# Attention in one kernel: score banks read in pairs, maxima read one bank at a time, VectorE turning the maxima

## The reference, cut to what matters

```python
q, k, v = (split_heads(binlinear(x, W, b)) for W, b in ((Wq, bq), (Wk, bk), (Wv, bv)))
att = jnp.einsum('bhtd,bhsd->bhts', q, k) * 8 ** -0.5
att = jax.nn.softmax(att, axis=-1)
y = jnp.einsum('bhts,bhsd->bhtd', att, v)
return binlinear(y.transpose(0, 2, 1, 3).reshape(8, 512, 128), Wp, bp)
```

## Time and profile before

| | us |
|---|---|
| median of 3 runs | 989.87 |
| lowest and highest | 982.49, 992.93 |
| the profiled execution | 992.35 |
| its span | 990.5 |
| attention of layer 0 in the span | about 30 to 439 |

### The profile page before, as it was taken

How to read it: one execution, slowest core, us unless ns; L and a number is a source line. 1 busy time by engine, 2 the same in 40 slices (tenths; PEclk the granted TensorE clock), 3 DMA queues, 4 the chain that set the end, 5 groups by cost and what they waited for, 6 DMA issues and landing times. The chain is left out here.

```text
span 990.5 us, 18391 instructions
## 1 busy us (share of the span) xinstructions
PE 897.2 (91%) x6674; PEld 461.9 (47%) x6674; DVE 695.5 (70%) x1054; ACT 634.7 (64%) x1383; POOL 366.1 (37%) x355
## 2 busy tenths in 40 slices
PE   4699999999999999979998989899769999999997
PEld 2333444344434344448888878332223444444443
DVE  7879888898989999613333338878867767766654
ACT  4468677778777878852322222476557778777875
POOL 4013030214343333005556542255645547554300
PEclk9579899999999999989999989999789999999999
DMA  7615525140414000036766553259977999999800
GB/s 226 250 39 207 230 71 211 40 162 27 176 45 151 28 26 25 8 98 181 209 198 199 164 176 96 54 111 136 144 88 75 108 110 101 103 104 112 92 12 22
DMA packets 80973, 114.30 MB, mean 115 GB/s; under 512 B 12946, under 2 KB 58004, under 8 KB 78452
## 3 DMA queue, kind: packets, MB, share of 16 engines
q1 hardware_dynamic: 73684, 94.87, 48.2%
q0 software_dynamic: 6352, 17.86, 5.3%
q10 hardware_dynamic: 848, 0.40, 0.1%
HBM read 56.00 MB, written 33.57 MB: 90 GB/s over the span
## 5 line engine op out<-in xcount | busy, mean ns | idle before, releaser
L989 DVE TENSOR_REDUCE a_nmax<-quad 128x2 f32<-128x1024 f32 x256 | 302.1, 1220 | 32.4 <-PE quad L603 29.9
L798 ACT ACTIVATE a_probs<-bank 128x512 f32<-128x512 f32 x339 | 190.8, 598 | 53.0 <-PE bank L620 36.9
L1873 ACT ACTIVATE a_late<-quad 128x256 f32<-128x256 f32 (+3 forms) x512 | 180.4, 461 | 37.3 <-PE quad L1642 36.6
L2028 DVE SCALAR_TENSOR_TENSOR a_late<-a_late,const 128x512 f32<-128x512 f32 x128 | 117.8, 928 | 73.8 <-ACT a_late L1873 73.5
L632 PE MATMUL av<-a_probs,a_va 128*32 128x256 f32 x2048 | 166.1, 397 | 0.9 <-ACT a_probs L798 0.6
L603 PE MATMUL quad<-k_stack,q_stack 24*128 24x512 f32 x512 | 133.6, 523 | 9.9 <-DVE a_nmax L989 5.8
L620 PE MATMUL bank<-q_stack,k_stack 26*128 26x512 f32 x339 | 136.8, 504 | 2.8 <-DMA q_stack<-a_nparts 2.0
L798 ACT ACTIVATE a_probs<-misc 128x512 f32<-128x512 f32 x173 | 103.4, 598 | 28.9 <-PE bank L620 16.2
L1642 PE MATMUL quad<-q_stack,k_stack 96*128 96x256 bf16 (+3 forms) x512 | 104.1, 305 | 7.4 <-ACT a_late L1873 3.7
L1653 PE MATMUL av<-a_late,a_va 128*32 128x512 f32 (+3 forms) x1024 | 96.1, 448 | 8.1 <-DVE a_late L2039 7.1
L508 POOL DMA_INDIRECT sorted_rows<-x_rows,a_slot x64 | 62.4, 974 | 107.5 <-PE av L632 105.0
(11 more groups left out here) (304 smaller groups left out, 1406.1 us busy)
## 6 DMA issues: line engine op xcount, KB each, us to landing
spread<-a_parts SPq DMA_DIRECT2D x48, 256.0 KB
q_stack<-a_parts SPq DMA_DIRECT2D x96, 128.0 KB, 7.4
k_stack<-a_parts SPq DMA_DIRECT2D x96, 128.0 KB, 7.8
wu<-packed_weights SPq DMA_DIRECT2D x20, 384.0 KB
m_wu<-packed_weights SPq DMA_DIRECT2D x19, 384.0 KB
q_stack<-spread SPq DMA_DIRECT2D x7, 1024.0 KB
k_stack<-spread SPq DMA_DIRECT2D x7, 1024.0 KB
sorted_rows<-in_shape_constants POOLq DMA_DIRECT2D x5, 1040.0 KB, 5.4
```

Source lines behind the costliest of these rows:

```text
L798: act.activation(probs[:, (GH * s + j) % 8, :], col_bank(n)[:, :], ACT.Exp, scale=scale).then_inc(col_free, 1)
L989: dve.tensor_reduce(nmax[quad % 2][:, at:at + 2 * TT:TT], row_slot(n)[:, :, :], AX_X, ALU.max, negate=True)\
L1873: act.activation(probs[:, (64 * b + n) % 12, kt * P:T], quad[:, n % 4, kt * P:T], ACT.Square, bias=1.0, scale=0.25)\
L2028: dve.scalar_tensor_tensor(out=blocks, in0=blocks, scalar=1.0, in1=S["tri"][:, None, :].broadcast_to([P, GH, P]), op0=ALU.add, op1=ALU.mul ...
```

## The change

Two ring layouts change places. The four banks of `quad` become two pairs that hold the scores, two heads each, and everything else that ScalarE reads; ScalarE takes both heads of a pair in one exponential of 1024 columns. The three single banks become the ring of the maxima, and VectorE reduces them one bank, 512 columns, at a time. TensorE waits ahead of each single maxima matmul. The turn of the maxima moves from TensorE to VectorE, which transposes blocks of 32 x 32 into `ntop`; there is one row of maxima per head in place of two, and SyncE writes them with four transfers of sixteen pieces of 128 bytes. It comes behind the first reduction of the next quad. AHEAD is 6. Gathers, projections, logits and counts now lie in the pair ring and are read by ScalarE; the reciprocal of the sums stays on VectorE one step later, the scaling and the bias go to GpSimd (`scale_rows`, `add_bias`), the last batch excepted. Two small matmuls of the start write into `av`. The two bookkeeping semaphores of each ring become `max_mm`, `max_free` and `unit_mm`, `unit_read`. The core of the diff:

```diff
-        nmax = [sb(f"nmax{i}", [P, P]) for i in range(2)]
-        nparts = sb("nparts", [DQ1, 2, P], F32R)
+        nmax = [sb(f"nmax{i}", [P, STRIP]) for i in range(2)]
+        ntop = [sb(f"ntop{i}", [P, STRIP]) for i in range(2)]
+        gathered = sb("gathered", [P, 2, NCOMP])
...
-        AHEAD = 8
+        AHEAD = 6
         STACK = 16 * 2
         WRITES = 16 * 2 * len(HALVES)
-        ROWS = 16 * 2 * GH
+        ROWS = 16 * GH
...
-        W1_AT = (-4, -3)
+        W1_AT = (-3, -2)
...
+        def pair_of(n):
+
+            return S["quad"][:, 2 * ((n - SINGLES) % 2):2 * ((n - SINGLES) % 2) + 2, :]
+
+        def bank_of(n):
+
+            return S["quad"][:, n % 4, :] if n < SINGLES else pair_of(n)[:, 0, :]
+
+        def wait_bank(engine, n):
+
+            if n < SINGLES:
+                wait(engine, unit_read, n - 3)
+            elif n < SINGLES + 2:
+                wait(engine, unit_read, SINGLES)
+            elif units[n - 2][0:2] == ("gather", B - 1):
+                wait(engine, last_read, units[n - 2][2] + 1)
+            else:
+                wait(engine, unit_read, n - 1)
+
+        def read_by_now(u):
...
-                wait(sp, row_free, row_no["turn", quad, 0] + 1)
-                for i in range(2 if quad else 1):
-                    for j in range(GH):
-                        row = STRIP * j + HROWS + i
-                        sp.dma_start(qs[b % 4][row:row + 1, c, :], nparts[TT * j:TT * (j + 1), i, :].bitcast(F32))\
-                          .then_inc(rows_in[quad % 2], 16)
+                wait(sp, turned, quad + 1)
+                rows = qs[b % 4][HROWS:HROWS + STRIP * (GH - 1) + 1:STRIP, c, :].rearrange("r (t q f) -> r t q f", t=TT, q=P // STRIP)
+                for q in range(P // STRIP):
+                    sp.dma_start(rows[:, :, q, :], ntop[quad % 2][STRIP * q:STRIP * q + TT * GH, :]).then_inc(rows_in[quad % 2], 16)
...
+            def scale_rows(b, u):
+                wait(pool, rec, 2 * b + u + 1)
+                if u == 0 and b >= 1:
+                    wait(pool, unit_mm, unit_no["y", b - 1, 0] + 1)
+                pool.tensor_tensor(yn[:, 2 * u:2 * u + 2, :].rearrange("p k (h d) -> p k h d", d=DH),
+                                   gathered[:, :, 0:C].rearrange("p k (h d) -> p k h d", d=DH),
+                                   rden[:, u, :, :, None].broadcast_to([P, 2, H, DH]), ALU.mult).then_inc(yn_done, 1)
+
+            def add_bias(b):
+                wait(pool, unit_read, unit_no["proj", b, 0] + 1)
+                rows = S["s"][:, TT * b:TT * (b + 1), :]
+                pool.tensor_tensor(rows, rows, S["bp"][:, None, :].broadcast_to([P, TT, C]), ALU.add)
...
+                if t - 1 in GATHER_AT and b >= 1:
+                    scale_rows(b - 1, GATHER_AT.index(t - 1))
                 if t in QK_AT and b + LEAD < B:
                     split_one(b + LEAD, QK_AT.index(t), (split_q, split_k)[QK_AT.index(t)])
+                if t == PROJECT_AT + 1 and b >= 1:
+                    add_bias(b - 1)
...
-                wait(pe, row_free, n - 1)
                 for k in range(2):
+                    n = GH * m + 2 * i + k
                     r = 2 * (1 - i) + k
                     at = slice(STRIP * r, STRIP * r + HROWS)
-                    last = pe.matmul(row_slot(n)[:, k, :], qs[b % 4][at, c, qt * P:(qt + 1) * P].bitcast(F32R),
-                                     ks[b % 4][at, c, :].bitcast(F32R), start=True, stop=True)
-                last.then_inc(row_mm, 1)
-
-            def turn(quad):
-                n = row_no["turn", quad, 0]
-                wait(pe, row_free, max(n - 1, row_no["max", TT * quad + TT - 1, 1] + 1))
-                pe.transpose(row_slot(n)[:, 0, 0:P], nmax[quad % 2][:, :], S["ident"]).then_inc(row_mm, 1)
-
-            def score(s, j):
-                n = col_no["s", s, j]
+                    wait(pe, max_free, n - 2)
+                    pe.matmul(max_banks[n % 3][:, :], qs[b % 4][at, c, qt * P:(qt + 1) * P].bitcast(F32R),
+                              ks[b % 4][at, c, :].bitcast(F32R), start=True, stop=True).then_inc(max_mm, 1)
+
+            def scores(s, i):
+                n = unit_no["s", s, i]
                 quad, kt = s // TT, s % TT
                 b, c = quad // NG, quad % NG
-                if kt == 0 and j == 0:
+                if kt == 0 and i == 0:
                     wait(pe, rows_in[quad % 2], ROWS * (quad // 2 + 1))
-                wait(pe, col_free, n - 2)
-                at = slice(STRIP * j, STRIP * j + HROWS + 2)
-                pe.matmul(col_bank(n)[:, :], ks[b % 4][at, c, kt * P:(kt + 1) * P].bitcast(F32R),
-                          qs[b % 4][at, c, :].bitcast(F32R), start=True, stop=True).then_inc(col_mm, 1)
+                wait_bank(pe, n)
+                for k in range(2):
+                    j = 2 * i + k
+                    at = slice(STRIP * j, STRIP * j + HROWS + 1)
+                    last = pe.matmul(pair_of(n)[:, k, :], ks[b % 4][at, c, kt * P:(kt + 1) * P].bitcast(F32R),
+                                     qs[b % 4][at, c, :].bitcast(F32R), start=True, stop=True)
+                last.then_inc(unit_mm, 1)
 
             def weigh(s, part):
 
                 b, c, kt = s // 16, s % 16 // TT, s % TT
                 if part == 0:
...
             for s in range(-AHEAD, 0):
                 maxima(s + AHEAD, 0)
-                if s + AHEAD == TT:
-                    turn(0)
                 maxima(s + AHEAD, 1)
-                if s in (-8, -7, -6):
-                    turn_x(s + 13)
+                if s < 3 - AHEAD:
+                    turn_x(s + AHEAD + 5)
                 if s in W1_AT:
                     turn_w1(W1_AT.index(s))
             for s in range(LAST):
                 b, t = s // 16, s % 16
-                score(s, 0)
-                score(s, 1)
+                scores(s, 0)
                 if s + AHEAD < LAST:
                     maxima(s + AHEAD, 0)
                 if s >= 1:
                     weigh(s - 1, 0)
-                score(s, 2)
-                score(s, 3)
+                scores(s, 1)
                 if s + AHEAD < LAST:
                     maxima(s + AHEAD, 1)
...
+            def exps(s, i):
+                n = unit_no["s", s, i]
+                if i == 0:
+
+                    wait(act, av_mm, s - 1)
+                wait(act, unit_mm, n + 1)
+                at = (GH * s + 2 * i) % 8
+                act.activation(probs[:, at:at + 2, :], pair_of(n), ACT.Exp, scale=scale).then_inc(unit_read, 1)
...
+            def read_gathered(b, u):
+                n = unit_no["gather", b, u]
+                wait(act, unit_mm, n + 1)
+                wait(act, yn_done, 2 * b + u)
+                act.activation(gathered[:, :, :], bank_of(n)[:, 0:2 * NCOMP].rearrange("p (k n) -> p k n", k=2), ACT.Copy).then_inc(unit_read, 1)
+
+            def read_projected(b):
+                n = unit_no["proj", b, 0]
+                wait(act, unit_mm, n + 1)
+                act.activation(S["s"][:, TT * b:TT * (b + 1), :], bank_of(n).rearrange("p (t c) -> p t c", t=TT), ACT.Copy).then_inc(unit_read, 1)
...
-                exps(s)
+                exps(s, 0)
+                exps(s, 1)
+                if t == 0 and b >= 1:
+                    read_o(b - 1, 1)
+                if t == 8:
+                    read_o(b, 0)
                 if s in GATES_AT:
                     store_gates(GATES_AT.index(s))
+                if s == LOGITS_AT:
+                    read_logits()
                 if s in FIRST_QK_AT:
                     read_qk(LEAD - 1, FIRST_QK_AT.index(s))
                 if s == 2 + ROUTE_AT:
                     act.wait_ge(route_step, 3)
                     act.activation(expo[:, :, :], shifted[:, :, :], ACT.Exp).then_inc(r_exponents, 1)
-                if t == 0 and b >= 1:
-                    read_o(b - 1, 1)
-                if t == 8:
-                    read_o(b, 0)
+                if t in GATHER_AT and b >= 1:
+                    read_gathered(b - 1, GATHER_AT.index(t))
                 if t == TURN_AT and b >= 1:
                     read_y(b - 1)
                 if t in QK_AT and b + LEAD < B:
                     read_qk(b + LEAD, QK_AT.index(t))
+                if t == PROJECT_AT and b >= 1:
+                    read_projected(b - 1)
+                if s == COUNT_AT:
+                    read_counts()
                 if t == VALUES_AT and b + 1 < B:
                     read_v(b + 1)
...
+            def maximum(m, k):
+                n, quad, qt = GH * m + k, m // TT, m % TT
+                at = TT * ((k + 2) % GH) + qt
+                wait(dve, max_mm, n + 1)
+                dve.tensor_reduce(nmax[quad % 2][:, at:at + 1], max_banks[n % 3][:, :], AX_X, ALU.max, negate=True).then_inc(max_free, 1)
+
+            def turn(quad):
+                wait(dve, max_free, GH * TT * (quad + 1))
+                wait(dve, rows_in[quad % 2], ROWS * (quad // 2))
```

(70 more changed lines are left out.)

317 lines of the change are left out of this document (133 added, 184 removed).

## The result

The changed kernel takes 1004.68 us (median of 4 runs, 1000.90 to 1009.86) against 989.68 us for the kernel before: ratio 1.0165, 95% interval 1.0089 to 1.0241, 15 us more. The forecast was 997 with a range of 974 to 1022. The time lies in the range; it is slower by over 1% (the interval begins at 0.9%), which I had given 0.38 behind 0.42 for "same". The profiled execution of the changed kernel took 1007.08 us, with a span of 1005.3. Ratios and mean clocks in this document leave out executions that took over 1.5% longer than the fastest of the same kernel in the same call.

What follows compares the result with a forecast made beforehand. VectorE was taken as the bound (2.28 us a step), with ScalarE (2.2) and TensorE (2.0) close. Terms summed to +7.3 on the profiled 992.35, less 2.5 to the median: 997 us, range 974 to 1022.

Steps and rivals of the forecast that it cites:

- Maxima in single banks: VectorE: 512 reductions of 512 columns spaced 0.60 us replace 256 of 1024 spaced 1.14: +15 us (0 to +36).
- Rival 3: VectorE: successive reductions do not overlap, 46 us more, so 1043 us; chance 0.03.
- The turn: Turning the maxima: one VectorE transpose, 0.21 us each, replaces TensorE's transpose, cast and subtraction, 0.68 each: -15 us.
- Inserts on TensorE: Matmuls for queries, keys, values and the turn of y starve VectorE about 0.94 us instead of 0.80: +4 us.
- projection: Output projection: its insert costs VectorE about 0.94 us where addition and gap took 1.07, seven times: -1 us.
- gathers: Gathers: scaling to GpSimd, read to ScalarE, but VectorE still starved 0.94 us plus a 0.27 reciprocal: -1 us.
- Copy of the output sums: ScalarE's copy comes after the step's exponentials, so the next sum waits 0.3 us, 15 times: +4.5 us (0 to 8).
- hand-overs: Bank hand-overs between TensorE and VectorE, twice as many with little slack, 0.02 us a step: +3 us (0 to 10).
- rival 4: Whole loop: gains and payments cancel and new waits hide behind each other, leaving about 985 to 990 us; chance 0.15.
- The end: After the last maxima, six steps at 2.19 us remain instead of eight at 2.25: -4.9 us.
- Rows of maxima, and AHEAD 8 to 6: Row transfers with the shorter lead: 11 late landings of 0.3 us, plus 1 for bulk transfers: +4.3 us.
- Rival 2: Rows of maxima come late at every quad, 32 x 0.9 us plus falls of the clock: 1030 us; chance 0.17.

Runs made afterwards that it cites:

- run 12: Kernel before with only the turn of the maxima moved to VectorE's transpose (one row, four transfers), repeated in a later call: ratio 0.9867.
- run 2: Kernel before with only the turn of the maxima moved to VectorE's transpose (one row, four transfers): ratio 0.9799, by the means 0.983.
- run 9: Changed kernel with AHEAD back at 8, in one call with the unedited changed kernel: ratio 0.9989 to the kernel before.
- run 11: Kernel before with VectorE's turn and each 1024-column reduction split into two of 512: ratio 0.9994.
- run 10: Changed kernel unedited (AHEAD 6), in one call with its AHEAD 8 version: ratio 1.0145 to the kernel before.
- run 7: Kernel before with VectorE's turn (one row, four transfers) and AHEAD 6 instead of 8: ratio 1.0368.
- run 6: Changed kernel with AHEAD 7 instead of 6: ratio 1.0114 to the kernel before.
- run 8: Changed kernel with four extra, overwritten score products per quad ahead of TensorE's wait for rows of maxima: ratio 1.0277 to the kernel before.
- run 1: Changed kernel with AHEAD back at 8 instead of 6, first measurement: ratio 0.9992 to the kernel before.
- run 4: Kernel before with AHEAD 6 instead of 8, eight row transfers and TensorE's turn kept: ratio 1.213, by the means 1.216.
- run 5: Changed kernel measured again with no edit: ratio 1.0136 to the kernel before.
- run 3: Kernel before with each 1024-column reduction split into two of 512 on the same banks: ratio 1.0103, by the means 1.0135.

## Why the prediction was right or wrong

- *Maxima in single banks*, +15: reductions of 679 to 680 ns spaced 0.60, both as worked out. In time +10 to +13, so a little over-sized; as a mechanism right. Rival 3, no overlap, would have meant 0.68 between starts and is out. The Trainium skill (VectorE: DVE Perf Modes, "The DRAIN you can't avoid") says that the next operation waits until the pipe is empty, and in the same paragraph that one that is not held starts earlier, which the prediction left out; the trace, with 0.60 between starts of operations of 0.68, agrees with the second.
- *The turn*, -15: -13 in run 12, -17 to -20 in run 2. The transpose lasts 0.20 but moves the next reduction by 0.12 only (201.25 to 201.37), not 0.21. Right in mechanism and size.
- *Inserts on TensorE*, +4, *projection*, *gathers*, *logits*: VectorE's idle behind a gather is mostly 0.90 or 1.02 (the first line below), behind the values 0.7 to 1.5, behind queries and keys 0.3 to 0.9, predicted 0.94 for all; behind the turn of y only about 0.4. The reciprocal lasts 0.34 and adds 0.25, predicted 0.27.
```profile
218.12 0.69 DVE L1035 TENSOR_REDUCE a_nmax<-bank 128x1 f32<-128x512 f32 x1 [1.02 <-PE misc L626]
...
367.10 0.34 DVE L1052 RECIPROCAL a_rden<-a_gathered 128x32 f32<-128x32 f32 x1
367.35 1.22 DVE L1035 TENSOR_REDUCE a_nmax<-bank 128x1 f32<-128x512 f32 x2
```
- *Copy of the output sums*, +4.5: 2.5 us in 11 waits; *hand-overs*, +3: not seen. With the other small terms I had +7.9 for what runs 9 and 11 measure as -0.5, within 5. Each small term counted a wait on one engine as time of the whole loop. That most of such waits fall into another engine's slack, rival 4's reasoning, fits the sum of -0.5 better; the terms were not run one by one.
- *The end*, -4.9: right. Score pairs of the last steps start at 431.31 and 433.50, 2.19 a step as worked out, and the gain of two steps shows as the loop's start at 50.6 instead of 55.7.
- *Rows of maxima, and AHEAD 8 to 6*, +4.3: **the step that failed**. The waits themselves were sized nearly well: 8 of them, 6.3 us, against 11 at 0.3 and 1 for bulk transfers. The last landing was said to be wanted at 4.8 and there at 5.1, and the four last waits are indeed 0.2 (the first at 303.87); the other four are 0.7 to 2.8. But I priced the clock at nothing in the sum, though the earlier trace rows showed it at half behind such a wait, and left it as a remark. By runs 9 and 10 the lead costs 15.5 net of the 5 won at the start, 20 gross where I had 4.3. Nor would a price for the clock behind late rows have been enough: only 14 of the 54 us at half clock follow such waits. Rival 2 had the right mechanism in part (late rows and falls of the clock, 1030 where every quad is late); run 7 shows that case, at 1.0368.
- *The clock's late falls* stood in no step. Why there are more of them with a lead of 6 or 7 than with 8 is open: run 6 has them without any wait for rows, run 8 has them with the waits covered, runs 9 and 12 have one of them with a lead of 8, run 11 three, and run 1 none. What sets them off was not isolated; the last section shows what comes ahead of them.

That the time came out in the forecast's own range, 990 to 1008, is luck in part: small terms too large by 8 us stood in for half of the lead's, too small by 16. The forecast was +7.3, and 15 were measured.

## What to carry to other kernels

A lead constant changed along with a rewrite is an edit of its own: measure it alone, first. Here it cost 1.6%, while the good part of the change, one VectorE transpose in place of a turn through TensorE with twice the transfers, is worth 1.3 to 2.0% by itself; the kernel before with that edit alone is the fastest of all those run (959.72 us against 976.72 on one chip, 978.57 against 991.36 on another).
Where several engines stand as close as here (2.0, 2.2 and 2.28 us a step), waits found on one need not add up to time; here the small ones did not, while a step at half clock took 3.47 us for 2.40. Read the clock column of the windows before adding up waits, and give it a term with its own range.

## What the runs showed of the hardware

TensorE's granted clock fell behind standstills that are not waits for a DMA. In run 6 TensorE's records stand without a gap from 208 to 218 us. TensorE, VectorE and the windows of run 6:
```profile
218.11 0.50 PE L639 MATMUL quad<-q_stack,k_stack 25*128 25x512 f32 x2
218.12 0.50 PE L626 MATMUL misc<-k_stack,q_stack 24*128 24x512 f32 x1
219.90 0.79 PE L626 MATMUL bank<-k_stack,q_stack 24*128 24x512 f32 x1 [1.29 <-DVE a_nmax L1035]
```
```profile
219.16 1.29 DVE L1035 TENSOR_REDUCE a_nmax<-bank 128x1 f32<-128x512 f32 x2 [1.50 <-PE misc L626]
```
```profile
218.00:219.00 1.00, 0.61 (x7) 0.19 (x3) 0.00 (x0) 0.00 (x0) 0.29 (x1) 1.00 0.17 58
219.00:220.00 1.00, 0.10 (x1) 0.10 (x1) 0.84 (x2) 0.88 (x1) 0.47 (x1) 0.93 0.03 8
220.00:221.00 1.00, 1.00 (x5) 0.38 (x9) 1.00 (x3) 1.00 (x2) 0.49 (x1) 0.50 0.00 0
```
Counted in order, the reduction at 219.16 reads the maxima matmul that is recorded at 216.81. That is 2.35 us later, where it is 0.60 otherwise, and ScalarE's exponentials are as late. VectorE and ScalarE stand still with it, TensorE then stands still for 1.29 us until a bank is read, and from about 219.9 us the clock is 0.50 (1.2 GHz). The same is seen ahead of the changed kernel's falls at 274 us (recorded at 271.70, read at 273.94) and 329 us (325.17 and 328.51). Starts and lengths of matmuls in a trace can be off, so that only their readers show that the results came late.

Runs 4 and 7 apart, where TensorE waits for rows, most falls after 200 us come within 3 us of the end of such a standstill of TensorE: 1.0 to 1.5 us ahead of all six in run 6, 2.1 in run 5, 1.0 and 2.0 in run 10, 1.2 twice and 0.9 in run 11, 1.3 in run 12, 0.8 in run 9. It is not a rule: in run 3 the clock fell at 353 and 387 us with no gap over 0.5 just ahead, and standstills of 1.0 us had no fall behind them (181.90 in the changed kernel). Whether the standstill brings the fall, or the late results and the fall have one cause, no run here shows.

The unchanged kernel before took 976.72, 994.56 and 991.36 us in three calls on three chips, with mean clocks of 0.964, 0.959 and 0.960; no chip was used twice, so chip and occasion aren't told apart. A difference of 1.8% between calls is as large as the effect studied here, so runs are compared only with those of the same call.
